# Graph network, last two edge passes: TensorE waits for a tabled count of landed tiles instead of for its own group's tiles

## The chip, the cores and the metric

The kernel runs on one core of a Trainium2 chip. The metric is the device time of one execution in microseconds (us); it is the median of several runs, and one further execution was taken with the hardware profiler, from which all rows of the trace come.

## What is computed

Four graph layers run on 6,250 nodes (256 features, float32) and 100,000 edges (`src`, `dst`; the edges come sorted by `dst`): two attention layers, a continuous-filter convolution, a relational layer and a gated normalised sum. The change touches the edge passes of the last two. In the reference they read

```python
# relation layer (L2)
hW = jnp.einsum('nd,rde->rne', h, weight)
msg = hW[edge_type, src]
m = jax.ops.segment_sum(msg, dst, num_segments=num_nodes)
...
# last layer (L3), row = src, col = dst
msg = gated[col] * edge_values[:, None]
out = jax.ops.segment_sum(msg, row, num_segments=n)
sumnorm = jax.ops.segment_sum(edge_values * r_D[col, 0], row, num_segments=n)
```

`src` is drawn evenly over the nodes; `dst` is 6250 times the square of an even draw, so that low node numbers have many edges and high ones few.

## The kernel before

The edges lie in TP = 784 tiles of P = 128, and the nodes in NT = 50 node tiles of 127. A scatter-add is done as a sum of matmuls: a tile of gathered rows (128 edges) is multiplied with a one-hot matrix that says for each edge which node of a node tile it goes to. A tile of edges that reaches into a new node tile is needed once for each of them; each such pair is a **slot**, and there are S = 832 slots. Slot s works for node tile nrow[s] and reads edge tile s - nrow[s], so slots run ahead of tiles by one with every new node tile: at the end slot 831 reads tile 782. Work goes in groups of GROUP = 8: NTG = 98 groups of tiles, NG = 104 groups of slots.

Both edge passes (`phase_rel_messages`, names `rel_...`, and `phase_source_sums`, names `so_...`, `source_ring`, `source_sums`) share one shape. Each engine has its own program, written out by hand, and semaphores tie them:

- ACT copies the row numbers of tile group g into `idx` (L2216, L2809), once the gather that used this buffer before has landed.
- POOL issues 8 indirect DMAs for tile group g (L2179, L2771) into a ring of RING = 12 (relation) or RING2 = 9 (last) groups. Its DMAs increment `x_ready[r]`. Before it overwrites a ring place it waits for `o_ready` of slot group g - LAG, with LAG = 5, or g - LAG2, with LAG2 = 2.
- VectorE (DVE) builds the one-hots of slot group g + 1 (L2231 in one instruction, L2834 in eight), then adds the 8 products of slot group g to the node sums (L2245, L2844). It loads 8 values of `nrow` into registers for each; the last pass does so twice a group, ahead of the one-hots and ahead of the adds, into one set of registers.
- TensorE (PE) in `sums(g)` loads 8 ring places from `tring` into registers, waits for the one-hots, and makes 8 products (L2198, L2789; a float32 product shows as two rows of weights and two of data). Each half group increments `o_ready`. In the relation pass three half-group PSUM buffers turn over, in the last pass 8 banks, one per slot, so that TensorE's first half there waits for the first four adds of the group before.

What sets the order around the change is this wait ahead of `sums(g)` on TensorE:

```python
pe.wait_ge(x_ready[r], it * (16 * GROUP) + 16 * GROUP)
sums(it * RING + r, r)
```

So slot group g waits until tile group g has landed, for all g below 98; the slot groups 98 to 103 wait for no tiles. When VectorE has made the last add, a block ends with all engines meeting, and the next phase starts (the gate's projection after the relation pass, `phase_last` after the last pass). VectorE also builds the tables `tring` and `nrow` in `phase_index` (by `dst`, for the relation pass) and `phase_order` (by `src`, for the last one).

Of the kernel before, what the change touches and what calls it, by code (L numbers as in the profile page):

```python
# [175 lines left out]
def phase_index(nc, m, d, sem):  # L176
# [15 lines left out]
    with ExitStack() as ctx:  # L192
# [25 lines left out]
        with nc.Block() as block:  # L218
# [12 lines left out]
            def _(dve):  # L231
# [76 lines left out]
                ch.link(nc.vector.tensor_tensor(ring[:, 0, :], ring[:, 0, :], ring[:, 1, :], ALU.add))  # L308
                ch.do(nc.vector.tensor_copy(m.tring[:, 0:S], ring[:, 0, :]))
                ch.do(nc.vector.tensor_copy(m.nrow[:, 0:S], tmp[0:1, :]))  # L310


                ch.do(nc.vector.tensor_copy(start[:], tmp[:, 0:S:P]))
# [1833 lines left out]
def phase_rel_messages(nc, m, d, x, sem):  # L2147
# [6 lines left out]
    x_ready = [sem(f"rows_gathered{b}") for b in range(RING)]  # L2154
    idx_ready = sem("index_ready")
    idx_pass = sem("index_pass")
    hot_ready = sem("onehot_ready")
    o_ready = sem("slot_sums")
    acc_done = sem("added")
# [2 lines left out]
    with ExitStack() as ctx:  # L2162
# [5 lines left out]
        with nc.Block() as block:  # L2168
# [15 lines left out]
            @block.tensor  # L2184
            def _(pe):
                regs = [pe.alloc_register(f"pe_rel_{j}") for j in range(GROUP)]

                def sums(g, r):
                    b = r % 2
                    pe.load(regs, m.tring[0:1, bass.ds(g * GROUP, GROUP)])  # L2190
                    ts = [pe.snap(t, min_val=0, max_val=RING * GROUP - 1) for t in regs]
                    pe.wait_ge(hot_ready, g + 1)
                    for j in range(GROUP):
                        n = g * PART + j // PER
                        q = (r * PART + j // PER) % BUFS
                        if j % PER == 0:
                            pe.wait_ge(acc_done, n * PER + PER)
                        ins = nc.tensor.matmul(psO[q][j % PER // (PER // 2)][:, j % (PER // 2), :], hot[b][:, j, :], x[:, bass.ds(ts[j] * D, D)], start=True, stop=True)  # L2198
                        if j % PER == PER - 1:
                            ins.then_inc(o_ready, 1)  # L2200
                with pe.Fori(0, NG // RING - 1) as it:
                    for r in range(RING):
                        pe.wait_ge(x_ready[r], it * (16 * GROUP) + 16 * GROUP)
                        sums(it * RING + r, r)
                for g in range(NG - NG % RING - RING, NG):
                    if g < NTG:
                        pe.wait_ge(x_ready[g % RING], g // RING * (16 * GROUP) + 16 * GROUP)
                    sums(g, g % RING)
                pe.wait_ge(o_ready, NG * PART)

            @block.scalar
            def _(act):
                def index(g, r, turn):
                    if not (isinstance(g, int) and g < RING):
                        act.wait_ge(x_ready[r], turn * (16 * GROUP))
                    nc.scalar.copy(idx[r][:], m.rel_tile[:, bass.ds(g * GROUP, GROUP)]).then_inc(idx_ready, 1)  # L2216
                tile_turns(act, index, 1)

            @block.vector
            def _(dve):  # L2220
# [495 lines left out]
def phase_source_sums(nc, m, d, x, sem):  # L2716
# [7 lines left out]
    rows_ready = sem("slot_rows_loaded")  # L2724
    idx_ready = sem("index_ready")
    idx_pass = sem("index_pass")
    places_ready = sem("places_spread")
    hot_ready = sem("onehot_ready")
    o_ready = sem("slot_sums")
# [14 lines left out]
    with ExitStack() as ctx:  # L2744
        sb, ps = buf_maker(nc, ctx, "so")
        edges = sb("edges", [P, TP * PAY])
        nrow = sb("nrow", [1, SR], I32)
        tring = sb("tring", [1, SR], I32)
        shift = sb("shift", [P, NT])
        places = sb("places", [P, NT, P])  # L2750
        idx = [sb(f"idx{b}", [P, GROUP], I32) for b in range(RING2)]
# [2 lines left out]
        with nc.Block() as block:  # L2754
# [21 lines left out]
            @block.tensor  # L2776
            def _(pe):
                regs = [pe.alloc_register(f"pe_so_{j}") for j in range(GROUP)]
                pe.wait_ge(rows_ready, 32)

                def sums(g, b):
                    pe.load(regs, tring[0:1, bass.ds(g * GROUP, GROUP)])
                    ts = [pe.snap(t, min_val=0, max_val=RING2 * GROUP - 1) for t in regs]
                    pe.wait_ge(hot_ready, g + 1)
                    for j in range(GROUP):
                        if j % PER == 0:

                            pe.wait_ge(acc_done, g * GROUP + j + PER)
                        ins = nc.tensor.matmul(psO[j][:, 0:K], hot[b][:, j, :], x[:, bass.ds(ts[j] * K, K)], start=True, stop=True)  # L2789
                        if j % PER == PER - 1:  # L2790
                            ins.then_inc(o_ready, 1)
                with pe.Fori(0, NTG // RING2 // 2) as it:
                    for r in range(2 * RING2):
                        pe.wait_ge(x_ready[r % RING2], it * (32 * GROUP) + (r // RING2 + 1) * (16 * GROUP))
                        sums(it * (2 * RING2) + r, r % 2)
                for g in range(NTG - NTG % (2 * RING2), NG):
                    if g < NTG:
                        pe.wait_ge(x_ready[g % RING2], (g // RING2 + 1) * (16 * GROUP))
                    sums(g, g % 2)
                pe.wait_ge(o_ready, NG * PART)  # L2800

            @block.scalar
            def _(act):
                act.wait_ge(order_ready, 16)

                def index(g, r, turn):
                    if not (isinstance(g, int) and g < RING2):
                        act.wait_ge(x_ready[r], turn * (16 * GROUP))
                    nc.scalar.copy(idx[r][:], edges[:, bass.ds(g * (GROUP * PAY), GROUP * PAY)].rearrange("p (j k) -> p j k", k=PAY)[:, :, 0]).then_inc(idx_ready, 1)  # L2809
                turns(act, index, 1)  # L2810

            @block.vector
            def _(dve):
                v = nc.vector
                regs = [dve.alloc_register(f"dve_so_{j}") for j in range(GROUP)]
                v.memset(m.sums[:], 0.0).then_inc(zeroed, 1)
                v.tensor_scalar(shift[:], m.iota[:, 0:NT], float(P), None, ALU.mult).then_inc(shift_ready, 1)
                dve.sem_inc(acc_done, GROUP)
                dve.wait_ge(shift_ready, 1)
                v.tensor_tensor(places[:], m.iota[:, 0:P].unsqueeze(1).to_broadcast([P, NT, P]), shift[:].unsqueeze(2).to_broadcast([P, NT, P]), ALU.add).then_inc(places_ready, 1)  # L2820
                dve.wait_ge(places_ready, 1)
                dve.wait_ge(zeroed, 1)
                dve.wait_ge(rows_ready, 32)
                dve.wait_ge(order_ready, 16)
                flat = places[:].rearrange("p n e -> p (n e)")

                def numbers(g):
                    dve.load(regs, nrow[0:1, bass.ds(g * GROUP, GROUP)])
                    return [dve.snap(n, min_val=0, max_val=NT - 1) for n in regs]

                def onehots(g, b, ns):
                    for j in range(GROUP):
                        t = nc.s_assert_within(g * GROUP + j - ns[j], 0, TP - 1, skip_runtime_bounds_check_because="buckets are numbered so that this is an edge tile's number")
                        ins = v.tensor_scalar(hot[b][:, j, :], flat[:, bass.ds(ns[j] * P, P)], edges[:, bass.ds(t * PAY + 2, 1)], edges[:, bass.ds(t * PAY + 1, 1)], ALU.is_equal, ALU.mult)  # L2834
                    ins.then_inc(hot_ready, 1)

                def adds(g, ns):
                    for j in range(GROUP):
                        if j % PER == 0:
                            dve.wait_ge(o_ready, g * PART + j // PER + 1)  # L2840

                        dve.wait_ge(acc_done, g * GROUP + j + GROUP)
                        to = m.sums[:, bass.ds(ns[j] * K, K)]
                        v.tensor_tensor(to, to, psO[j][:, 0:K], ALU.add).then_inc(acc_done, 1)  # L2844

                def group(g, b, more=True):

                    if more:
                        onehots(g + 1, 1 - b, numbers(g + 1))
                    adds(g, numbers(g))  # L2850
                onehots(0, 0, numbers(0))
                with dve.Fori(0, NG // 2 - 1) as it:
                    for b in range(2):
                        group(it * 2 + b, b)
                group(NG - 2, 0)
                group(NG - 1, 1, False)
                dve.wait_ge(acc_done, S + GROUP)

# [125 lines left out]
def build(nc, d, w, out):  # L2984
    m = Mem()
    with ExitStack() as ctx:
        def sb(name, shape, dt=F32):
            return ctx.enter_context(nc.sbuf_tensor(name, shape, dt))
# [12 lines left out]
        def eb(name, shape, dt=F32):  # L3001
            return edge_ctx.enter_context(nc.sbuf_tensor(name, shape, dt))
        m.loc = eb("loc", [P, SX])
        m.tring = eb("tring", [1, SX], I32)
        m.nrow = eb("nrow", [1, SX], I32)
        m.pos = eb("pos", [P, TP], I32)
        m.pay = eb("pay", [P, TP, PAY])

# [161 lines left out]
```

## Time and profile before

| | us |
|---|---|
| runs | 7715.18, 7710.42, 7712.72 |
| median | 7712.72 |
| profiled execution, its own time | 7716.48 |
| its span, first to last instruction | 7714.7 |
| relation pass, first gather to last add | 5289.1 to 6316.9 |
| last pass, first gather to last add | 6479.2 to 7532.8 |
| busy over the span: PE, DVE, ACT, POOL | 5501.5, 4562.5, 1960.2, 4805.4 |

The spans of the two passes are read from the first row of the gathers and the last row of the adds. Together they take 27% of the time. An engine is counted busy only while an instruction of it computes or, for POOL, describes a DMA; a register load, a semaphore wait and a branch leave no row and show as idle time ahead of the next row, whose releaser is then "issue" or whatever semaphore came last.

### The profile page before, as it was taken

What the parts mean: (1) busy time and instruction counts of PE and PEld (TensorE: products, weight loads), DVE (VectorE), ACT (ScalarE), POOL (GpSimd) and SP (SyncE); (2) the same over time, 40 slices, a digit from 0 to 9 for tenths busy, and PEclk for the clock granted to TensorE, in tenths of its full rate; (3) what the DMA queues carried; (4) which work ended last, traced back from release to release, by engine and by line L of the source; (5) the groups of instructions that cost most, each with busy time, mean ns of one, the idle gap of its engine ahead of it and who ended that gap; (6) DMA issues with size and microseconds to landing.
All of it is one profiled execution on the core that took longest, in us unless ns stands there. A gap on an engine that the chain in (4) does not pass through costs nothing. (4 is left out here: it accounts for less than half of the span.)

```text
span 7714.7 us, 103020 instructions
## 1 busy us (share of the span) xinstructions
PE 5501.5 (71%) x21382; PEld 3803.1 (49%) x21383; DVE 4562.5 (59%) x9626; ACT 1960.2 (25%) x6454; POOL 4805.4 (62%) x4886
## 2 busy tenths in 40 slices
PE   5768999977699999675677778995565554565550
PEld 2235565544566555454666664443444443444440
DVE  5357777777577777767344443223444456666667
ACT  0036666632366666332000001110000001000002
POOL 0017777765477777655777776777777733777750
PEclk8578999986889999866555557997777777777775
DMA  0075455522345545223111112433333323333322
GB/s 17 25 164 143 136 135 135 136 73 63 122 133 135 135 134 137 59 66 91 31 31 31 31 31 76 125 118 103 105 105 105 105 87 117 106 105 105 105 76 69
DMA packets 431408, 733.88 MB, mean 95 GB/s; under 512 B 112552, under 2 KB 278777, under 8 KB 429718
## 3 DMA queue, kind: packets, MB, share of 16 engines
q0 software_dynamic: 212352, 484.47, 24.0%
q1 hardware_dynamic: 217510, 246.12, 10.5%
q14 instruction: 141, 1.16, 0.1%
q8 instruction: 57, 0.93, 0.1%
q10 hardware_dynamic: 1348, 1.21, 0.0%
HBM read 610.03 MB, written 121.40 MB: 95 GB/s over the span
## 5 line engine op out<-in xcount | busy, mean ns | idle before, releaser
L746 POOL DMA_INDIRECT at_x<-table,at_idx x1664 | 1575.6, 947 | 587.8 <-issue 525.6
L821 PE MATMUL at_psO<-at_x,at_main 128*128 128x273 f32 x3328 | 1032.2, 434 | 157.3 <-DVE agg L1011 156.7
L1242 POOL DMA_INDIRECT order<-pay,pos x784 | 823.1, 1050 | 391.1 <-issue 245.0
L2789 PE MATMUL so_psO<-source_ring,so_hot 128*128 x1664 | 603.8, 540 | 489.2 <-issue 381.4
L2771 POOL DMA_INDIRECT source_ring<-gated_rows,so_idx x784 | 749.0, 955 | 286.5 <-issue 232.7
L2023 POOL DMA_INDIRECT conv_x<-conv_table,conv_idx x784 | 755.7, 964 | 263.7 <-issue 238.7
L2198 PE MATMUL rel_psO<-rel_ring,rel_hot 128*128 x1664 | 596.6, 536 | 449.4 <-issue 257.6
L2179 POOL DMA_INDIRECT rel_ring<-rel_table,rel_idx x784 | 741.3, 946 | 250.5 <-issue 237.9
L821 PEld LDWEIGHTS at_psO<-at_x,at_main 128*128 128x128 f32 x3328 | 606.3, 200 | 529.7 <-issue 412.1
L1011 DVE TENSOR_TENSOR agg<-agg,at_psO 128x273 f32 x1664 | 725.7, 436 | 221.6 <-DVE agg L1011 169.3
L2789 PEld LDWEIGHTS so_psO<-source_ring,so_hot 128*128 128x128 f32 x1664 | 458.9, 283 | 634.0 <-issue 531.4
L2198 PEld LDWEIGHTS rel_psO<-rel_ring,rel_hot 128*128 128x128 f32 x1664 | 455.7, 281 | 590.6 <-issue 492.2
L2245 DVE TENSOR_TENSOR rel_sums<-rel_sums,rel_psO 128x256 f32 x832 | 350.0, 421 | 449.5 <-PE rel_psO L2198 350.6
L907 ACT COPY at_row<-at_psO 1x273 f32<-1x273 f32 x1664 | 523.3, 373 | 345.9 <-PE at_psO L821 345.6
L1002 DVE TENSOR_TENSOR at_x<-at_x,at_psE 128x512 f32<-128x512 f32 x832 | 560.8, 674 | 0.8 <-issue 0.8
L2844 DVE TENSOR_TENSOR source_sums<-source_sums,so_psO 128x257 f32 x832 | 351.9, 423 | 245.1 <-PE so_psO L2789 135.4
L2060 PE MATMUL conv_psO<-conv_msg,conv_hot 128*128 x1664 | 381.8, 421 | 157.7 <-DVE conv_hot L2099 149.5
L2047 PE MATMUL conv_psF<-w_radial,conv_attr 12*128 12x64 f32 x1568 | 359.2, 419 | 161.7 <-DVE conv_prod L2109 134.0
L2060 PEld LDWEIGHTS conv_psO<-conv_msg,conv_hot 128*128 128x128 f32 x1664 | 362.8, 331 | 176.6 <-issue 176.3
L2047 PEld LDWEIGHTS conv_psF<-w_radial,conv_attr 12*128 12x128 f32 x1568 | 341.3, 326 | 179.6 <-DVE conv_prod L2109 131.9
L799 PE MATMUL at_psA<-a_ij,at_fullT 128*128 x3328 | 402.5, 257 | 0.0
L799 PEld LDWEIGHTS at_psA<-a_ij,at_fullT 128*128 128x128 f32 x3328 | 395.0, 195 | 0.0
(487 smaller groups left out, 8292.5 us busy)
## 6 DMA issues: line engine op xcount, KB each, us to landing
at_place<-places SPq DMA_DIRECT2D x208, 256.0 KB, 3.7
rel_table<-cr_rows SPq DMA_DIRECT2D x50, 1024.0 KB
at_x<-table,at_idx POOLq DMA_INDIRECT x1664
pj_x<-table SPq DMA_DIRECT2D x20, 640.0 KB, 4.2
order<-pay,pos POOLq DMA_INDIRECT x784, 2.1
conv_x<-conv_table,conv_idx POOLq DMA_INDIRECT x784, 2.4
rel_ring<-rel_table,rel_idx POOLq DMA_INDIRECT x784, 2.7
source_ring<-gated_rows,so_idx POOLq DMA_INDIRECT x784, 2.8
```

The costliest lines, as they stand in the source:

```text
L746: pool.indirect_dma_start(x[b][:, j, 0:TABW], None, d.table[0:NR, :], bass.IndirectOffsetOnAxis(ap=idx[b][:, j:j + 1], axis=0)).then_inc(x ...
L799: nc.tensor.matmul(psA[:, j, :], fullT[:, j, :], m.a_ij[:, bass.ds(ns[j] * (2 * H) + H, H)], start=False, stop=False, skip_group_check=True)
L821: ins = nc.tensor.matmul(psO[j % BANKS][:, 0:AGG], main[b % 2][:, j, :], x[b][:, j, 0:AGG], start=True, stop=True)
L1011: nc.vector.tensor_tensor(to, to, psO[j % BANKS][:, 0:AGG], ALU.add).then_inc(acc_done, 1)
L1242: pool.indirect_dma_start(d.order[0:TP * P, :], bass.IndirectOffsetOnAxis(ap=m.pos[:, t:t + 1], axis=0), m.pay[:, t, :], None).then_inc(pl ...
L2023: pool.indirect_dma_start(x[b][:, j, :], None, d.conv_table[:, :], bass.IndirectOffsetOnAxis(ap=idx[b][:, j:j + 1], axis=0)).then_inc(x_re ...
L2047: ins = nc.tensor.matmul(psF[b][:, j, :], attr[b][:, j * P:(j + 1) * P], m.w_radial[:], start=True, stop=True)
L2060: ins = nc.tensor.matmul(psO[b][j // (GROUP // 2)][:, j % (GROUP // 2), :], hot[b][:, j, :], msg[:, bass.ds(ts[j] * K, K)], start=True, st ...
L2179: pool.indirect_dma_start(x[:, at:at + D], None, d.rel_table[:, :], bass.IndirectOffsetOnAxis(ap=idx[r][:, j:j + 1], axis=0)).then_inc(x_r ...
L2198: ins = nc.tensor.matmul(psO[q][j % PER // (PER // 2)][:, j % (PER // 2), :], hot[b][:, j, :], x[:, bass.ds(ts[j] * D, D)], start=True, st ...
L2771: pool.indirect_dma_start(x[:, at:at + K], None, d.gated[:, :], bass.IndirectOffsetOnAxis(ap=idx[r][:, j:j + 1], axis=0)).then_inc(x_ready ...
L2789: ins = nc.tensor.matmul(psO[j][:, 0:K], hot[b][:, j, :], x[:, bass.ds(ts[j] * K, K)], start=True, stop=True)
```

## The change

A new table `needed` has one number for each slot group: how many edge tiles must have landed before all its 8 slots can be computed. That is the tile of its last slot plus one (slot number + 1 - nrow). The relation pass's table is written in `phase_index`, the last pass's at the start of `phase_source_sums`. ACT, which waited for each gather to land before it copied the next row numbers over that buffer, now also adds 8 to a new semaphore `gathered` after each such wait, and goes on doing so for the last ring of tile groups. TensorE no longer waits on `x_ready`; it loads `needed[g]` into a register and waits for `gathered` to reach it. In the last pass TensorE's loop is now 52 turns of two slot groups (before: 5 turns of 18, and 14 groups written out), and VectorE keeps the node tile numbers of a group in one of two sets of registers from the one-hots to the adds, so that they are loaded once.

```diff
--- before.py
+++ after.py
...
+                ch.do(nc.vector.tensor_scalar(m.needed[:], slot[0:1, 3, GROUP - 1:S:GROUP], 1.0, None, ALU.add))
...
+    gathered = sem("tiles_gathered")
...
                 def sums(g, r):
                     b = r % 2
                     pe.load(regs, m.tring[0:1, bass.ds(g * GROUP, GROUP)])
+                    tiles = pe.value_load(m.needed[0:1, bass.ds(g, 1)], min_val=1, max_val=TP)
                     ts = [pe.snap(t, min_val=0, max_val=RING * GROUP - 1) for t in regs]
                     pe.wait_ge(hot_ready, g + 1)
+                    pe.wait_ge(gathered, tiles)
                     for j in range(GROUP):
                         n = g * PART + j // PER
...
                 with pe.Fori(0, NG // RING - 1) as it:
                     for r in range(RING):
-                        pe.wait_ge(x_ready[r], it * (16 * GROUP) + 16 * GROUP)
                         sums(it * RING + r, r)
                 for g in range(NG - NG % RING - RING, NG):
-                    if g < NTG:
-                        pe.wait_ge(x_ready[g % RING], g // RING * (16 * GROUP) + 16 * GROUP)
                     sums(g, g % RING)
                 pe.wait_ge(o_ready, NG * PART)
 
             @block.scalar
             def _(act):
-                def index(g, r, turn):
-                    if not (isinstance(g, int) and g < RING):
-                        act.wait_ge(x_ready[r], turn * (16 * GROUP))
+                def index(g, r):
                     nc.scalar.copy(idx[r][:], m.rel_tile[:, bass.ds(g * GROUP, GROUP)]).then_inc(idx_ready, 1)
-                tile_turns(act, index, 1)
+
+                def landed(r, turn):
+
+                    act.wait_ge(x_ready[r], turn * (16 * GROUP) + 16 * GROUP)
+                    act.sem_inc(gathered, GROUP)
+                for r in range(RING):
+                    index(r, r)
+                with act.Fori(0, NTG // RING - 1) as it:
+                    for r in range(RING):
+                        landed(r, it)
+                        index(it * RING + r + RING, r)
+                for g in range(NTG - NTG % RING - RING, NTG):
+                    landed(g % RING, g // RING)
+                    if g + RING < NTG:
+                        index(g + RING, g % RING)
 
...
+    gathered = sem("tiles_gathered")
+    need_ready = sem("needed_tiles")
...
+        needed = sb("needed", [1, NG], I32)
...
+                pe.wait_ge(need_ready, 1)
 
                 def sums(g, b):
                     pe.load(regs, tring[0:1, bass.ds(g * GROUP, GROUP)])
+                    tiles = pe.value_load(needed[0:1, bass.ds(g, 1)], min_val=1, max_val=TP)
                     ts = [pe.snap(t, min_val=0, max_val=RING2 * GROUP - 1) for t in regs]
                     pe.wait_ge(hot_ready, g + 1)
+                    pe.wait_ge(gathered, tiles)
...
-                with pe.Fori(0, NTG // RING2 // 2) as it:
-                    for r in range(2 * RING2):
-                        pe.wait_ge(x_ready[r % RING2], it * (32 * GROUP) + (r // RING2 + 1) * (16 * GROUP))
-                        sums(it * (2 * RING2) + r, r % 2)
-                for g in range(NTG - NTG % (2 * RING2), NG):
-                    if g < NTG:
-                        pe.wait_ge(x_ready[g % RING2], (g // RING2 + 1) * (16 * GROUP))
-                    sums(g, g % 2)
+                with pe.Fori(0, NG // 2) as it:
+                    for b in range(2):
+                        sums(it * 2 + b, b)
                 pe.wait_ge(o_ready, NG * PART)
...
-                regs = [dve.alloc_register(f"dve_so_{j}") for j in range(GROUP)]
+                regs = [[dve.alloc_register(f"dve_so{b}_{j}") for j in range(GROUP)] for b in range(2)]
...
+                v.scalar_tensor_tensor(out=needed[:], in0=m.iota[0:1, GROUP - 1:S:GROUP], scalar=1.0, in1=nrow[:, GROUP - 1:S:GROUP], op0=ALU.add, op1=ALU.subtract).then_inc(need_ready, 1)
...
-                def numbers(g):
-                    dve.load(regs, nrow[0:1, bass.ds(g * GROUP, GROUP)])
-                    return [dve.snap(n, min_val=0, max_val=NT - 1) for n in regs]
+                def numbers(g, b):
+                    dve.load(regs[b], nrow[0:1, bass.ds(g * GROUP, GROUP)])
+                    return names(b)
+
+                def names(b):
+                    return [dve.snap(n, min_val=0, max_val=NT - 1) for n in regs[b]]
...
                 def group(g, b, more=True):
 
                     if more:
-                        onehots(g + 1, 1 - b, numbers(g + 1))
-                    adds(g, numbers(g))
-                onehots(0, 0, numbers(0))
+                        onehots(g + 1, 1 - b, numbers(g + 1, 1 - b))
+                    adds(g, names(b))
+                onehots(0, 0, numbers(0, 0))
                 with dve.Fori(0, NG // 2 - 1) as it:
                     for b in range(2):
                         group(it * 2 + b, b)
...
+        m.needed = eb("needed", [1, NG], I32)
```

On TensorE, at the start of the loop of the last pass, these rows stood from the loop's head to the first product of a slot group (`so_tring`: ring places; ISA rows are waits, register moves and address work, without names):

```order
L2792 ISA
L2782 ISA
L2782 TENSOR_LOAD so_tring
L2783 ISA
L2788 REGISTER_ALU
L2789 ISA
L2789 MATMUL so_psO<-source_ring,so_hot 128x257
```

and these stand there now:

```order
L2811 ISA
L2799 TENSOR_LOAD so_tring
L2800 ISA
L2800 TENSOR_LOAD so_needed
L2800 ISA x2
L2801 ISA
L2807 REGISTER_ALU
L2808 ISA
L2808 MATMUL so_psO<-source_ring,so_hot 128x257
```

The wait that stood ahead of the load of `so_tring` is gone, and a second load (`so_needed`) stands between it and the first product. The relation pass reads the same with `rel_...` names.

On VectorE, in the last pass, from the last one-hot of group g + 1 to the first add of group g, the rows were:

```order
L2834 TENSOR_SCALAR so_hot<-so_places,so_edges 128x128
L2828 ISA
L2828 TENSOR_LOAD so_nrow
L2829 ISA
L2840 REGISTER_ALU
L2842 REGISTER_ALU
L2844 ISA
L2844 TENSOR_TENSOR source_sums<-source_sums,so_psO 128x257
```

and are now:

```order
L2864 TENSOR_SCALAR so_hot<-so_places,so_edges 128x128
L2859 ISA
L2870 REGISTER_ALU
L2872 ISA
L2874 ISA
L2874 TENSOR_TENSOR source_sums<-source_sums,so_psO 128x257
```

The second load of `so_nrow` is gone; the one ahead of the one-hots stays.

## Rows read from the trace of the kernel before

**Rows 1.** Costliest groups, relation pass: us busy, mean ns, idle before, releasers.

```profile
L2179 POOL DMA_INDIRECT rel_ring<-rel_table,rel_idx x784 | 741.3, 946 | 250.5 <-issue 237.9 <-ACT rel_idx L2216 12.0 <-PE rel_psO L2198 0.6
```

**Rows 2.** Timeline, relation pass: start, length (us), engine, [idle before <-releaser].

```profile
5303.18 5.51 PE L2198 MATMUL rel_psO<-rel_ring,rel_hot 128*128 x16 [37.43 <-DVE rel_hot L2231]
...
6100.75 0.20 ACT L2216 COPY rel_idx<-rel_tile 128x8 int32 x1 [9.82 <-DMA rel_ring<-rel_table,rel_idx]
6101.85 5.40 PE L2198 MATMUL rel_psO<-rel_ring,rel_hot 128*128 x16 [4.59 <-issue]
6105.60 4.36 DVE L2245 TENSOR_TENSOR rel_sums<-rel_sums,rel_psO 128x256 f32 x8 [3.58 <-PE rel_psO L2198]
6111.87 5.40 PE L2198 MATMUL rel_psO<-rel_ring,rel_hot 128*128 x16 [4.61 <-DVE rel_hot L2231]
```

**Rows 3.** Timeline, the end of the relation pass.

```profile
6261.84 5.40 PE L2198 MATMUL rel_psO<-rel_ring,rel_hot 128*128 x16 [4.65 <-DVE rel_hot L2231]
6265.06 2.11 DVE L2245 TENSOR_TENSOR rel_sums<-rel_sums,rel_psO 128x256 f32 x4 [3.56 <-PE rel_psO L2198]
...
6267.96 0.95 POOL L2179 DMA_INDIRECT rel_ring<-rel_table,rel_idx  x1 [0.30 <-issue]
6269.98 1.22 DVE L2231 TENSOR_TENSOR rel_hot<-rel_psI,loc 128x1024 f32<-128x1024 f32 x1 [0.47 <-issue]
...
6273.33 8.59 PE L2198 MATMUL rel_psO<-rel_ring,rel_hot 128*128 x32 [6.08 <-issue]
...
6295.59 4.01 PE L2198 MATMUL rel_psO<-rel_ring,rel_hot 128*128 x16 [0.63 <-DVE rel_hot L2231]
...
6301.62 4.01 PE L2198 MATMUL rel_psO<-rel_ring,rel_hot 128*128 x16 [2.03 <-DVE rel_hot L2231]
...
6314.82 2.11 DVE L2245 TENSOR_TENSOR rel_sums<-rel_sums,rel_psO 128x256 f32 x4 [0.21 <-DVE rel_sums L2245]
6321.29 0.39 SPq L2606 DMA_DIRECT2D ga_wsup<-in_s_W  x1
```

**Rows 4.** Costliest groups, last pass.

```profile
L2771 POOL DMA_INDIRECT source_ring<-gated_rows,so_idx x784 | 749.0, 955 | 286.5 <-issue 232.7 <-ACT so_idx L2809 48.0 <-PE so_psO L2789 5.8
```

**Rows 5.** Timeline, the end of the last pass.

```profile
7449.71 5.42 PE L2789 MATMUL so_psO<-source_ring,so_hot 128*128 x16 [4.51 <-issue]
...
7459.69 5.88 PE L2789 MATMUL so_psO<-source_ring,so_hot 128*128 x16 [4.56 <-issue]
...
7465.85 0.94 POOL L2771 DMA_INDIRECT source_ring<-gated_rows,so_idx  x1 [0.30 <-issue]
...
7471.13 5.30 PE L2789 MATMUL so_psO<-source_ring,so_hot 128*128 x16 [5.55 <-issue]
...
7490.03 3.07 DVE L2834 TENSOR_SCALAR so_hot<-so_places,so_edges 128x128 f32 x8 [0.96 <-issue]
7493.97 0.42 DVE L2844 TENSOR_TENSOR source_sums<-source_sums,so_psO 128x257 f32 x1 [0.87 <-issue]
...
7499.70 3.06 DVE L2834 TENSOR_SCALAR so_hot<-so_places,so_edges 128x128 f32 x8 [1.35 <-issue]
7503.73 4.38 DVE L2844 TENSOR_TENSOR source_sums<-source_sums,so_psO 128x257 f32 x8 [0.97 <-issue]
...
7509.07 3.07 DVE L2834 TENSOR_SCALAR so_hot<-so_places,so_edges 128x128 f32 x8 [0.97 <-issue]
...
7524.94 5.42 PE L2789 MATMUL so_psO<-source_ring,so_hot 128*128 x16 [4.20 <-DVE source_sums L2844]
7528.34 2.12 DVE L2844 TENSOR_TENSOR source_sums<-source_sums,so_psO 128x257 f32 x4 [1.32 <-PE so_psO L2789]
7530.67 2.12 DVE L2844 TENSOR_TENSOR source_sums<-source_sums,so_psO 128x257 f32 x4 [0.21 <-DVE source_sums L2844]
```

**Rows 6.** Timeline, the start of the last pass.

```profile
6486.22 6.82 DVE L2820 TENSOR_TENSOR so_places<-iota,so_shift 128x6400 f32<-128x6400 f32 x1
6486.84 7.03 POOL L2771 DMA_INDIRECT source_ring<-gated_rows,so_idx  x1 [0.30 <-issue]
...
6498.45 5.24 PE L2789 MATMUL so_psO<-source_ring,so_hot 128*128 x16 [61.07 <-DVE so_hot L2834]
```

**Rows 7.** VectorE's small operation nearest in size to the new ones.

```profile
7540.04 0.19 DVE L2938 TENSOR_SCALAR la_no_node<-mask 128x49 f32<-128x49 f32 x1 [7.24 <-PEq L2754]
```

More of the change, by code:

```diff
@@ L2804, in _, with index, landed @@
                 act.wait_ge(order_ready, 16)
-                def index(g, r, turn):
-                    if not (isinstance(g, int) and g < RING2):
-                        act.wait_ge(x_ready[r], turn * (16 * GROUP))
+                def index(g, r):
                     nc.scalar.copy(idx[r][:], edges[:, bass.ds(g * (GROUP * PAY), GROUP * PAY)].rearrange("p (j k) -> p j k", k=PAY)[:, :, 0]).then_inc(idx_ready, 1)
-                turns(act, index, 1)
+                def landed(r, turn):
+                    act.wait_ge(x_ready[r], turn * (16 * GROUP) + 16 * GROUP)
+                    act.sem_inc(gathered, GROUP)
+                for r in range(RING2):
+                    index(r, r)
+                with act.Fori(0, NTG // RING2 - 1) as it:
+                    for r in range(RING2):
+                        landed(r, it)
+                        index(it * RING2 + r + RING2, r)
+                for g in range(NTG - NTG % RING2 - RING2, NTG):
+                    landed(g % RING2, g // RING2)
+                    if g + RING2 < NTG:
+                        index(g + RING2, g % RING2)
             @block.vector
```

## The prediction

> **What bounds the kernel now.** I read first the grouped instructions of the two edge passes. In the relation pass POOL issues 784 gathers; their busy time and the idle time ahead of them, without the 12.0 us of the start, make (741.3 + 238.5) / 784 = 1.250 us each, 10.0 us per tile group [rows 1]. Almost all of that idle time is "issue", 0.3 us between two gathers; for TensorE's progress POOL waited 0.6 us in all in the relation pass and 5.8 us in the last pass [rows 1, 4]. So both passes run at POOL's pace, and nothing that TensorE or VectorE does sooner changes the start of a gather.
>
> Next I read the timeline in the middle. ACT is released by a landing at 6100.75, TensorE starts its group at 6101.85, works 5.40 us and starts the next at 6111.87: its turn is POOL's 10.0 us, and it is idle for 4.6 us of it. VectorE's adds follow 3.75 us behind TensorE's start and take 4.36 us [rows 2]. Both engines idle in every turn, and nothing there is on the path but the gathers.
>
> That ends with the last gather. In the relation pass it is issued at 6267.96; TensorE starts slot group 97 at 6273.33, and the groups 98 to 103 still follow: VectorE's last add ends at 6314.82 + 2.11 = 6316.93, and 4.4 us later the next phase issues its first load [rows 3]. So 43.6 us of the pass are a tail of seven groups at 6.03 us (TensorE's starts at 6295.59 and 6301.62). In the last pass the last gather is issued at 7465.85, group 97 starts at 7471.13 and the last add ends at 7530.67 + 2.12 = 7532.79: a tail of 61.7 us [rows 5]. Its pace is VectorE's: the adds of two groups in succession start at 7493.97 and 7503.73, the one-hots at 7490.03, 7499.70 and 7509.07, so 9.5 us a group on average. That is eight one-hots 3.07, eight adds 4.38, and two gaps, 0.87 to 0.97 ahead of the adds and 0.96 to 1.35 ahead of the one-hots, where the registers are loaded (1.35 with the loop's branch).
>
> **What the change does to the tails.** A slot group needs its last slot's number + 1 - nrow tiles. The node tiles follow from the reference's draws. For the relation pass (by dst) the slots 807, 815, 823 and 831 work for the node tiles 46, 47, 48 and 49, so the groups 100 to 103 need 762, 769, 776 and 783 tiles, which is 96, 97, 97 and 98 tile groups. For the last pass (by src) nrow is 47, 48, 48 and 49, which gives 761, 768, 776 and 783 tiles: 96, 96, 97 and 98 groups. Today slot group g waits for tile group g. In the middle of a pass TensorE only works further ahead in slots, which buys nothing while POOL sets the pace. At the last landing only slot group 103 is left for certain, where seven are left now.
>
> **Relation pass, worked forward.** Slot group 101 needs the 97th tile group, for which TensorE starts at 6261.84 today; its adds go from 6265.06 to 6269.5, and the one-hots of 103 from 6269.98 to 6271.2, all as in today's rows of another group [rows 3]. TensorE ends group 101 at 6267.2. It then loads registers twice; one load is hidden in 0.63 us today (the idle time at 6295.59), so I take 1.3 us for both, and group 102 starts at 6268.5, its adds 3.2 us later (6265.06 - 6261.84), from 6271.7 to 6276.2. TensorE is free at 6273.9, the last tiles have landed at about 6272.3 (1.0 us before today's start at 6273.33, as ACT's row stands 1.1 us ahead of TensorE's in the middle [rows 2]), and group 103 starts at 6275.2. Its adds run from 6278.4 to 6282.9. Against 6316.93 that is **34.0 us** less. Bounds: if each load costs TensorE what it costs VectorE at most (0.97 us, none hidden), three groups lose 1 us each, 31; if the second costs nothing, 36.
>
> **Last pass, worked forward.** Slot group 100 needs the 96th tile group, TensorE's start at 7449.71 today [rows 5]. Its adds start 3.4 us later (7528.34 - 7524.94), at 7453.1, and end at 7457.6. VectorE then loads once (0.96), makes the one-hots of 102 until 7461.7, and without the second load adds group 101 from 7461.9 to 7466.3; one-hots of 103 from 7467.3 to 7470.4; adds of 102 from 7470.6 to 7475.0. TensorE's group 103 needs the first four of these added, so it starts at 7473.0 (the last tiles have landed by 7470.1, 1.0 us before today's 7471.13), its adds begin 3.4 us later and take 4.45: the end is at 7480.8. Against 7532.79 that is **52.0 us** less. For this VectorE must keep up before: with one gap it needs 3.07 + 4.38 + 0.96 to 1.35 + 0.2, about 8.8 us a group, while 104 slot groups in the time of 98 tile groups ask for one in 10.0 x 98 / 104 = 9.4. It can. Where two slot groups hang on one landing it falls behind by 8.8 us and makes 1.2 us good with each following landing, which takes 8 groups; such pairs are 17 groups apart. If the removed load saves nothing, VectorE goes at 9.5 against 9.4 asked for and is never clear of the backlog: 87 groups at 9.52 behind the first 17 at 10.0 put the last add near 7493, 40 us less. Upper bound 54, with TensorE's group 103 starting on the landing.
>
> **What it adds.** Per slot group one register load and one more semaphore wait on TensorE, behind which stand only its own products. They lie in its idle 4.6 us, except in the tails, where they are counted. The landing now reaches TensorE over ACT; ACT is idle 9.8 of 10.0 us [rows 2], and TensorE's first load has moved ahead of the wait, so this is no later than today. ACT's own waits are the same landings as before, so POOL gets its numbers at the same time. Two small VectorE operations: the table in the index phase is on the path and costs what an operation on 49 elements does, 0.19 us [rows 7]. The one in the last pass delays the first one-hots by as much, which the second landing hides. At the start of that pass there is one more thing to see: while VectorE built `so_places` from two tables in SBUF (6.82 us), a gather took 7.03 us instead of 0.955 [rows 6, 4]. The new operation there is of the same kind but has 104 elements, so it can hold POOL for 0.2 us at most, between 0 and 0.2 of the path. The Trainium skill (SBUF — State Buffer, Who interferes with whom) says that a two-input VectorE operation with both inputs in SBUF contends with GpSimd for the shared ports, and that tensor_scalar can too. The trace agrees on the long operation; it does not on the 832 one-hots, beside which the gathers' mean stays at 0.955. By the rule a one-hot of 0.38 us (3.07 / 8) that met a gather would hold it too, but their number does not change, so neither does the sum.
>
> **Sum.** 34.0 + 52.0 - 0.2 - 0.1 = 85.7 us. The profiled execution took 7716.48 and would take 7630.8; the median of the runs is 3.8 us below it, so 7627.
>
> **Rivals.** (1) *VectorE's cadence in the last pass does not fall*, since the gap ahead of the adds is a wait or an issue time that stays without the load. For it: that gap also shows a semaphore wait for TensorE in places. Against it: it is 0.87 to 0.97 in the tail, where TensorE is done. The last pass gives 40 instead of 52: 7639. (2) *TensorE becomes the bound*, the case on the slower side. The second load and a wait on a register's value would have to stretch its turn. It works 5.4 us and idles at least 0.63 in the tail, 6.0 together; the 104 turns of the relation pass lie between 5303.18 and 6316.93, 9.75 us each, and those of the last pass between 6498.45 and 7532.79, 9.95 each [rows 2, 3, 5, 6]. If a turn comes to more than that, the pass is slower than today; at 10.75 us they lose 104 and 83 us, 7900. That asks for over 3.7 us more per turn, where a load on VectorE shows 0.97. (3) *The shorter loop.* TensorE's loop in the last pass goes back 52 times instead of 5. On VectorE, which has such a loop, the branch shows as 1.35 against 0.96, 0.4 us [rows 5]; on TensorE two turns have 2 x (9.95 - 6.0) = 7.9 us to spare, and a stall of 10 us at each branch would cost 52 x 2.1 = 109 us in that pass, which with the 34 of the other makes 7788. The Trainium skill (Runtime: NRT & Kernel Launch, Instruction fetch mechanics) says that a taken branch out of the fetched window stalls the engine until its target is fetched; VectorE's 0.4 us says that a loop of two groups does not pay that here. (4) *The change does not do what it says*: the count reaches TensorE late in the tail, or slot group 103 is not the only one left, and the tails stay: 7713.
>
> **Chances and range.** The forecast 0.82, rival 1 0.10, rival 2 0.03, rival 3 0.02, rival 4 0.03. The bounds of the forecast give 31 + 40 to 36 + 54, so 7623 to 7642; with 3 us of scatter between runs (7710.42 to 7715.18) 7620 to 7643, which leaves out the rivals 2 to 4 and little else. Since about 0.2%, 15 us, is what a measurement of this kernel can tell from no change: faster 0.92, same 0.03, slower 0.05.
>
> **What would show it.** Right: POOL still at 1.25 us a gather; between the last landing and the last add about 11 us in either pass (now 44 and 62); no idle time of more than 0.3 us ahead of the adds in the last pass's backlog; TensorE twice a pass two groups in succession without waiting. Wrong: a gap ahead of L2874 that stays near 0.9 (rival 1), TensorE's turns without idle time (2), idle time in every second turn (3), or POOL waiting for TensorE by more than the 0.6 and 5.8 us of now, which would move every later gather.

## The result and the profile after

The changed kernel takes 7633.68 us (median of 4 runs, 7627.78 to 7634.63) against 7711.57 us for the kernel before (4 runs): ratio 0.9898, 95% interval 0.9881 to 0.9915, 78 us less. Forecast were 7627 and 86 us less. The same kernel, run once more among the experiments, took 7619.66 us (ratio 0.9884, 0.9867 to 0.9900). The profiled execution has a span of 7632.6 us, 82.1 less than before.

The grouped instructions of the two passes say whether the gathers kept their pace, the first row as in [rows 1], the last as in [rows 4]:

```profile
L2181 POOL DMA_INDIRECT rel_ring<-rel_table,rel_idx x784 | 742.4, 947 | 250.6 <-issue 236.8 <-ACT rel_idx L2215 12.0 <-PE rel_psO L2202 1.8
...
L2787 POOL DMA_INDIRECT source_ring<-gated_rows,so_idx x784 | 750.0, 957 | 286.1 <-issue 238.0 <-ACT so_idx L2821 47.5 <-PE so_psO L2808 0.6
```

They did: (742.4 + 250.6 - 12.0) / 784 = 1.251 us each, and POOL waits for TensorE 1.8 and 0.6 us in all, where it was 0.6 and 5.8. The end of the relation pass in the timeline, against [rows 3]:

```profile
6264.40 9.25 PE L2202 MATMUL rel_psO<-rel_ring,rel_hot 128*128 x32 [4.62 <-DVE rel_hot L2244]
...
6271.36 0.94 POOL L2181 DMA_INDIRECT rel_ring<-rel_table,rel_idx  x1 [0.30 <-issue]
...
6277.49 5.40 PE L2202 MATMUL rel_psO<-rel_ring,rel_hot 128*128 x16 [3.84 <-issue]
...
6283.04 2.11 DVE L2258 TENSOR_TENSOR rel_sums<-rel_sums,rel_psO 128x256 f32 x4 [0.85 <-PE rel_psO L2202]
6292.52 0.39 SPq L2619 DMA_DIRECT2D ga_wsup<-in_s_W  x1
```

Slot groups 101 and 102 run back to back on one landing (32 rows in one piece; they start 3.04 us after the issue of the last gather that they need), and only group 103 follows the last landing. From the last gather's issue to the last add's end there are 13.8 us now, where there were 49.0. But the next phase's first load comes 7.4 us after the last add, not 4.4. The end of the last pass, against [rows 5]:

```profile
7421.54 7.55 PE L2808 MATMUL so_psO<-source_ring,so_hot 128*128 x24 [4.54 <-ACTq L2826]
...
7430.28 3.07 DVE L2864 TENSOR_SCALAR so_hot<-so_places,so_edges 128x128 f32 x8 [0.97 <-issue]
...
7433.59 4.39 DVE L2874 TENSOR_TENSOR source_sums<-source_sums,so_psO 128x257 f32 x8 [0.24 <-issue]
...
7444.77 2.00 PE L2808 MATMUL so_psO<-source_ring,so_hot 128*128 x8 [3.49 <-DVE source_sums L2874]
...
7449.50 2.12 DVE L2874 TENSOR_TENSOR source_sums<-source_sums,so_psO 128x257 f32 x4 [0.21 <-DVE source_sums L2874]
7458.72 0.37 SPq L2929 DMA_DIRECT2D la_a<-in_s_a  x1
```

The gap ahead of the adds is 0.24 us instead of 0.87, and group 103 waits for VectorE's adds, no longer for a landing. The last gather there is issued at 7438.46, so 13.2 us are left of 66.9.

I read the same marks (first and last gather, last add, next phase's first load) in every profile and cut the span by them. "Tail" is the stretch from the last gather's issue to the last add's end, "gate" the phase between the two passes:

| us | first gather at | gathers | tail | to next load | gate | gathers | tail | to next load | rest |
|---|---|---|---|---|---|---|---|---|---|
| before | 5289.1 | 978.9 | 49.0 | 4.4 | 157.9 | 986.6 | 66.9 | 7.2 | 174.7 |
| changed | 5291.3 | 980.1 | 13.8 | 7.4 | 158.3 | 987.6 | 13.2 | 7.1 | 173.9 |
| changed, again | 5282.9 | 978.7 | 12.8 | 5.1 | 156.6 | 986.7 | 13.2 | 7.1 | 174.1 |

The tails give 35.2 + 53.8 = 89.0 us. Back go 3.0 at the end of the relation pass, 2.2 in the two stretches of gathers and 2.2 ahead of the first one; the other columns together give 0.5 more, which makes 82.1. Of the 2.2 us ahead of the first gather only 0.2 can be the change's (its new table operation in the index phase took 0.23 us): that mark stands between 5278.3 and 5291.3 over the twelve profiles of this study, and the one of the changed kernel was the latest. Scatter in that part, which the change hardly touches, is also 8.4 of the 15.5 us between the two profiles of the changed kernel, whose medians are 7633.7 and 7619.7.

### The profile page after: what moved, and what is told of

It reads as the page before. It is cut to its first block and busy times, and to the rows that moved or that the text cites. A ratio compares the mean times of both kernels' runs of the same rounds, so it can differ in the third digit from the quotient of the medians.

```text
span 7632.6 us, 104169 instructions
## 1 busy us (share of the span) xinstructions
PE 5462.2 (72%) x21382; PEld 3774.1 (49%) x21383; DVE 4560.7 (60%) x9628; ACT 1962.9 (26%) x6454; POOL 4813.3 (63%) x4886
## 3 DMA queue, kind: packets, MB, share of 16 engines
q1 hardware_dynamic: 217510, 246.12, 10.5%
## 5 line engine op out<-in xcount | busy, mean ns | idle before, releaser
L2808 PE MATMUL so_psO<-source_ring,so_hot 128*128 x1664 | 584.6, 525 | 455.1 <-ACTq L2826 270.0
L2181 POOL DMA_INDIRECT rel_ring<-rel_table,rel_idx x784 | 742.4, 947 | 250.6 <-issue 236.8
L2202 PE MATMUL rel_psO<-rel_ring,rel_hot 128*128 x1664 | 576.9, 522 | 437.6 <-ACTq L2220 222.3
L1012 DVE TENSOR_TENSOR agg<-agg,at_psO 128x273 f32 x1664 | 725.2, 436 | 222.3 <-DVE agg L1012 169.1
L2808 PEld LDWEIGHTS so_psO<-source_ring,so_hot 128*128 128x128 f32 x1664 | 442.2, 273 | 597.5 <-issue 501.7
```

The source lines that it names most:

```text
L1012: nc.vector.tensor_tensor(to, to, psO[j % BANKS][:, 0:AGG], ALU.add).then_inc(acc_done, 1)
L2181: pool.indirect_dma_start(x[:, at:at + D], None, d.rel_table[:, :], bass.IndirectOffsetOnAxis(ap=idx[r][:, j:j + 1], axis=0)).then_inc(x_r ...
```

## Experiments

**The kernel again.** No edit.

> The changed kernel once more, unedited, to learn how far its time and its parts repeat. 7630 to 7636. In its trace: last gather to last add about 14 us in the relation pass and 13 us in the last pass, and from the last add to the next phase's first load 7.4 and 7.1 us. If the 3 us that the relation pass's end lost against before (4.4 to 7.4) are scatter, they differ here; if they come from TensorE now ending only 2.3 us ahead of VectorE, with POOL's 9.2 us drain behind it, they stand again.

Measured 7619.66, outside what I expected. Tails 12.8 and 13.2 us, and 5.1 us to the next load. So the tails repeat within about 1 us. The end of the relation pass's block, 3.0 us longer than before in the first profile, is 0.8 us longer here. What sets it is in the rows of the block's end (line of the block's `with`), for the kernel before, the changed one, and the repeat, in this order: engine queue, operation, length in ns, start in us.

```profile
L2168 POOLq DRAIN  x1: 9194/9194/9194, 6311.9 to 6311.9; - x1
...
L2168 DVEq DRAIN  x1: 17/17/17, 6317.2 to 6317.2; - x1
L2168 SPq EVENT_SEMAPHORE  x1: 17/17/17, 6321.2 to 6321.2; - x1
```

```profile
L2170 POOLq DRAIN  x1: 9194/9194/9194, 6283.1 to 6283.1; - x1
...
L2170 DVEq DRAIN  x1: 17/17/17, 6285.4 to 6285.4; - x1
L2170 SPq EVENT_SEMAPHORE  x1: 17/17/17, 6292.4 to 6292.4; - x1
```

```profile
L2170 POOLq DRAIN  x1: 9194/9194/9194, 6270.1 to 6270.1; - x1
L2170 DVEq DRAIN  x1: 17/17/17, 6274.6 to 6274.6; - x1
```

POOL waits for the last product, and only then drains, for 9.2 us; the engines are released when that ends (6311.9 + 9.2 = 6321.1, 6283.1 + 9.2 = 6292.3). VectorE is done 2.3 to 5.3 us after the drain starts and waits for it. So the block ends 9.4 us after TensorE's last product, as long as the adds end within that time. It holds beyond these three: in the ten profiles of kernels in which POOL waits for the last product, the next phase's first load comes 9.6 us after that product in all twenty block ends, while the adds end 2.3 to 5.3 us after it. What differs between the two profiles is when TensorE ends, 11.5 us after the last gather's issue in the first and 8.3 in the repeat: the last landing was counted after 5.9 against 4.3 us, and the 16 products of group 103 took 5.40 us at a mean granted clock of 0.72 (part of them at the 1.2 GHz level) against 3.72 us at 1.00 (2.4 GHz).

**The old numbers through the new table.** Relation pass (the last pass likewise):

```diff
-ch.do(nc.vector.tensor_scalar(m.needed[:], slot[0:1, 3, GROUP - 1:S:GROUP], 1.0, None, ALU.add))
+ch.do(nc.vector.tensor_scalar(m.needed[:], m.iota[0:1, GROUP - 1:S:GROUP], 1.0, float(TP), ALU.add, ALU.min))
```

> Everything of the change stays (table, count on ACT, register wait, short loop, two register sets), but the table holds what the wait of before asked for: 8 (g + 1) tiles, at most 784. If the gain is in the numbers of the table, it is gone: the seven slot groups stand behind the last landing again. Kept are some 5 us, since the last pass's tail of seven groups goes at 8.8 instead of 9.5 us, and 0.8 us of reaction per pass: 7703 to 7707. If the loop, the loads or the way of waiting carried the gain: near 7634.

Measured 7705.11 (ratio 0.9994, 0.9984 to 1.0004). The tails are back, 47.9 and 62.7 us. So the gain is in the numbers, but for the 4.2 us that are left (in the tails 1.1 and 4.2); the second load, the register wait, the hop over ACT and the loop of two groups cost nothing that shows.

**One pass alone.** The other pass's function is that of the kernel before.

> Only the relation pass is changed, the last pass is that of before. Theory of two separate tails: last gather to last add falls by 35 us, and the end of the block gives 3 back, so 32 less, 7679 to 7681. If the passes shared the gain in another way (an earlier phase that meets other work), the two halves would not add up to 78 us.

> Only the last pass is changed, the relation pass is that of before. Two separate tails: 54 us less in this one, nothing given back, 7657 to 7659, and together with the relation pass alone the whole 78 to 85 us. Otherwise they do not add up.

Measured 7677.54 (ratio 0.9960) and 7654.11 (0.9930). Measured beside them, the kernel before had 7709.34 and the changed one 7619.66. The two passes alone give 31.8 and 55.2 us, together 87.0 (I had expected 78 to 85); both at once give 89.7. They add up to within 2.7 us, less than the scatter of the phases ahead. In the profiles the relation pass's tail is 12.3 us with 5.4 to the next load, the last pass's 14.2 us.

**VectorE loads twice again.**

```diff
-                    adds(g, names(b))
+                    adds(g, numbers(g, b))
```

> The changed kernel, but VectorE in the last pass loads the node tile numbers again ahead of the adds. If the load is the 0.9 us gap there, VectorE goes at 9.5 us a group, 9.4 are asked for, its backlog is never worked off, and the last add comes 8 to 12 us later: 7642 to 7646. If the gap was a wait that needs no load, the time stays at 7634.

Measured 7632.31, below the 7642 to 7646 that I expected. Against the changed kernel's 7619.66 that is 12.7 more, against its first 7633.68 nothing, so the medians don't decide; the profiles do. The last pass's tail is 24.6 us, against 13.2 in both profiles of the changed kernel and 14.1 with the long loop below; the other parts agree within the scatter (gathers 978.8 and 987.0, relation tail 12.6). In its timeline the gap is back, and the adds that wait behind it are late:

```profile
7430.63 3.07 DVE L2864 TENSOR_SCALAR so_hot<-so_places,so_edges 128x128 f32 x8 [0.97 <-issue]
7434.57 0.42 DVE L2874 TENSOR_TENSOR source_sums<-source_sums,so_psO 128x257 f32 x1 [0.87 <-issue]
```

The gap is the load (0.87 against 0.24 us), and 0.6 us per group are worth 11.5 us at the end, because without them VectorE clears its backlog between two pairs of slot groups and with them it does not: ahead of the last pass's products TensorE waited 16 times for a landing and 90 times for VectorE's adds, in the changed kernel 65 and 46 times.

**The registers alone**, in the kernel before:

> The kernel before with one part of the change: VectorE's two register sets in the last pass, one load a group. POOL sets the pace, so only the tail of seven groups gains, 7 x 0.7 = 5 us: 7706. If VectorE's loads had held the pass up in the middle: 50 us or more less. If the gap was no load: 7711.

Measured 7706.96 (0.9998, 0.9988 to 1.0007), no difference that can be told. In the profile the last pass's tail falls from 66.9 to 63.6 us, 3.3 of the 5 expected. Only five of the seven turns have the load on the path, those between the first adds of group 97 and of group 102: 44.3 us instead of 47.6, 8.9 instead of 9.5 a turn. Ahead of the adds of groups 97 and 103 VectorE waits for TensorE in either kernel (2.9 and 1.6 us, before 2.8 and 1.3), and the load is hidden there. One edit is worth 3 us before the new counts and 11 behind them.

**TensorE's long loop**, 5 turns of 18 slot groups and 14 groups written out, in the changed kernel:

> The changed kernel with TensorE's loop of the last pass as before: 5 turns of 18 slot groups and 14 groups written out, instead of 52 turns of two. If the branch and the fetch behind it hide in TensorE's idle 4 us: no difference, 7631 to 7637. If the short loop costs something at each of its 52 branches that reaches the path, this is faster by that; if it saves fetches of code that held the gathers or the landings up, it is slower by a few us.

Measured 7627.05 (7619.46 to 7627.66), below the 7631 to 7637 that I expected and between the two medians of the changed kernel; tails 12.6 and 14.1 us, gathers 986.9 us. No cost of the short loop reaches the path: the stall of the rule that the prediction weighed (the Trainium skill, Runtime: NRT & Kernel Launch, Instruction fetch mechanics) does not show here.

**One tile group later.** All entries of both tables 8 higher, at most 784.

> The changed kernel with every entry of both tables 8 tiles higher, at most 784, so that each slot group waits for one tile group more than it needs. Theory of the tails: nothing in the middle; in the relation pass the slot groups 101, 102 and 103 all hang on the last landing, two more turns of 6.0 us behind it, 12 us; in the last pass 102 and 103, one more turn of 8.8 less the 2 us by which VectorE is late now, 7 us. 7634 + 19 = 7653. If a later count delayed the whole pass by one turn of the gathers: 10 us in each, and the tails as long as now.

Measured 7702.09, not 7653: nearly the whole gain was gone. The tails did about what was expected (23.8 and 25.1 us, 10 to 11 more in the first where I had 12, and 12 more in the second where I had 7), but the last pass's gathers took 1046.1 us instead of 986.7, which I had not looked for. The waits of its last pass, and POOL's timeline in its first turns:

```profile
POOL source_ring L2789 <- PE so_psO L2810: 63.1, 14, 6.9
```

```profile
6551.03 0.95 POOL L2789 DMA_INDIRECT source_ring<-gated_rows,so_idx  x1 [6.92 <-PE so_psO L2810]
...
6567.61 0.94 POOL L2789 DMA_INDIRECT source_ring<-gated_rows,so_idx  x1 [6.89 <-PE so_psO L2810]
...
6584.15 0.95 POOL L2789 DMA_INDIRECT source_ring<-gated_rows,so_idx  x1 [6.85 <-PE so_psO L2810]
```

POOL now waits for TensorE before a gather group, 6.9 us each time, so that a turn takes 16.6 us instead of 10.0. The cause is the ring: gather group g may start when slot group g - 2 has its first half (LAG2 = 2), and with the higher entry that slot group needs tile group g - 1 landed, so gathers and products alternate instead of overlapping. It lasts from group 9, the first that reuses a ring place, to about group 17, where the slots have run one group ahead of the tiles. Nine times 6.9 is 62 of the 63.1 us. In the relation pass, with LAG = 5, the gathers stayed at 979.0. In these first 17 groups the needed counts, in whole tile groups, are still the old ones (the slots have not yet run ahead by 8 tiles), so the wait of before had less than one tile group of slack there, and the change keeps it.

**POOL leaves early.** Without the last line of POOL's program in both passes:

```diff
                 turns(pool, gather, 1)
-                pool.wait_ge(o_ready, NG * PART)
```

> The changed kernel without POOL's last wait in both passes (for the last products); all engines still meet at the end of the block, and VectorE's last wait stands. Theory: POOL's drain of 9.2 us now starts only behind the last product and ends 7 us after the last add, in both passes; without the wait it starts behind the last gather, runs beside TensorE's and VectorE's last groups, and the next phase starts 0.3 to 0.5 us after the last add: 7 us less in either pass, 7619 to 7621. Rival: the drain waits for something that only ends with the block (or for the landings, and then takes 9.2 us from there): no change, or 3 us less.

> The kernel before without the same two waits. The relation pass ended 4.4 us after its last add there, the last pass 7.2 us. Theory: both fall to 0.3 to 0.5 us, 4 + 7 = 11 us less, 7700 to 7702. Rival as for the changed kernel: no change.

Measured 7609.20 (7608.46 to 7610.94; ratio 0.9870, 0.9854 to 0.9885), the fastest here, and for the kernel before 7697.53 (0.9983, 0.9974 to 0.9992), 12.8 less than the 7710.28 measured beside it (by the two block ends of the profiles 3.9 + 6.7 = 10.6). Both lie below what I expected, 7619 to 7621 and 7700 to 7702; the first expectation went out from 7634. In both, both blocks end 0.5 us after the last add. The relation pass's end with the wait gone, in the changed kernel:

```profile
L2170 POOLq DRAIN  x1: 24197/24197/24197, 6246.9 to 6246.9; - x1
...
L2170 DVEq DRAIN  x1: 17/17/17, 6274.4 to 6274.4; - x1
L2170 SPq EVENT_SEMAPHORE  x1: 17/17/17, 6274.6 to 6274.6; - x1
```

The drain begins while gathers are still being issued and ends at 6246.9 + 24.2 = 6271.1, 3.3 us ahead of VectorE's: hidden. But it does not get cheaper. The last gather's row is

```profile
6260.93 0.95 POOL L2181 DMA_INDIRECT rel_ring<-rel_table,rel_idx  x1 [0.30 <-issue]
```

It ends at 6260.93 + 0.95 = 6261.88, 9.2 us before the drain does, and so it is in all four blocks without the wait (both kernels, both passes): the drain takes 9.2 us from the end of POOL's last gather, or from the end of its wait where it has one. It does not count from the landings (here ACT counts the last at 6265.7), as my rival had it. Against the changed kernel the gain is 10.5 us by medians of two separate measurements (7619.66 and 7609.20), not the 14 of my expectation, which took the block end of 7.4 us from the first profile. By the profiles the two block ends give 4.6 + 6.6 = 11.2 us against the repeat, and the tails were 0.5 and 1.9 us longer in this execution.

## Why the prediction was right, and where it was off

The direction, the mechanism and the size held: POOL sets the pace, the middle of the passes gains nothing, and all of the gain but some 4 us is slot groups that no longer stand behind the last landing. The old numbers through the new table take it away again, which shows it.

*Relation pass, 34.0 us.* Measured 35.2 between the last gather and the last add (13.8 us left; the working gave 14.9), 36.2 in the repeat. The term of 1.3 us for two register loads on TensorE was wrong in size: groups 101 and 102 follow each other with no gap at all, and group 103 starts 0.2 us after ACT has counted the last landing (6277.3). And the working let TensorE start as late after a landing as before, where it starts 0.8 us sooner (below). In this one profile the last landing was counted 5.9 us after the last gather's issue (seven of the other profiles: 4.1 to 4.8), which ate part of that.

*The step that failed* is "VectorE's last add ends at 6314.82 + 2.11 = 6316.93, and 4.4 us later the next phase issues its first load", which I took as a constant behind the tail. It is not one: the block ends 9.4 us after TensorE's last product, because POOL waits for that product and then drains for 9.2 us. Before, VectorE's adds ended 5.3 us behind the last product and hid more than half of it. Now, at 2.3 and in the repeat 4.5 us behind it, less is hidden, so 3.0 of the 35.2 us went back (0.8 of the 36.2 in the repeat). It was not in my sum, nor in a rival. From the last gather to the next load, which is what counts, the pass gave 32.2 and 35.4 us. That the forecast of 34.0 lies between them is partly luck: what the working left out here lengthens the time, and the two terms above that it took too large shorten it.

*Last pass, 52.0 us.* Measured 53.8. The working put the last add at 15.0 us behind the last gather's issue, it is 13.2. Of the 1.8 us, 0.8 are TensorE's earlier start of group 103 (6.3 us behind the last gather, in the working 7.1), and 1.0 its products: the adds begin 2.4 us after that start, not the 3.4 taken from the kernel before, where the 16 products of the last group took 5.42 us at a mean granted clock of 0.69; now each half took 2.00 us, at 1.00. The pace without the second load was taken as 8.8 us and is 8.9 (the mean of 8.7 and 9.1 in the profile of the registers alone).

*What it adds, 0.3 us.* The operation in the last pass took 0.33 us, not 0.2, and the one in the index phase 0.23, not 0.19. The first delays nothing: the first one-hot starts 1.02 us after `so_places` is done, before and now, and the gather that `so_places` held ends 0.8 us after it in both. The gathers' stretches were 1.2 and 1.0 us longer in the first profile, and in the repeat 0.2 shorter and 0.1 longer: scatter.

*Rival 1* (VectorE's cadence does not fall, 12 us of the gain) had its price right, 11.5 us, and its condition wrong: the gap was the load. With the load back the tail is 42.3 us shorter than before, where the rival had 40. *Rivals 2 and 3* (TensorE as the bound, the short loop) did not come about; TensorE has idle time before nearly every group. The wait for the landing now shows as one for ACT's count, 222.3 us in 54 waits in the relation pass:

```profile
PE rel_psO L2202 <- ACTq L2220: 222.3, 54, 6.3
```

TensorE starts 3.04 us after the issue of the last gather that it needs (6264.40 after a gather one turn of 10.0 us ahead of the one at 6271.36), where it took 3.87 (6261.84 after the one a turn ahead of 6267.96 [rows 3]). It is so all along the pass: over the starts of the relation pass with more than 3 us of idle time ahead of them the median is 3.13 us (92 starts), and was 3.95 (98). So the hop over ACT costs less than having the load ahead of the wait saves; no run has the one without the other. "No later than today" in the working was 0.8 us too careful.

Of the signs, "about 11 us in either pass" between the last landing and the last add came out as about 8 and 9, for the same terms. "Twice a pass two groups in succession" was a slip: 104 slot groups hang on 98 tile groups, which makes six such pairs a pass.

My claim that nothing TensorE or VectorE does sooner changes the start of a gather held for this change. What TensorE does later is another matter, and I had not looked there: the shift by one tile group cost 59 us of gathers in the last pass.

## What to carry to other kernels

When a producer runs at a fixed pace through a ring, ask how many consumer steps stand behind its last item, and whether each truly needs it: seven groups, at 6 and 9 us, were worth 1.0 to 1.2% here, and the middle nothing. A wait by need also has to be checked from the other side, where the producer waits for the consumer: one tile group of unneeded lateness cost 59 us through a lag of two. And read the queues' own rows at the end of a block (drain, branch, semaphore), not the last busy row: the engine that finishes last may be one that only waited.

## What the runs showed that I had not expected

POOL's drain at the end of a block with 784 gathers takes 9.19 us (both passes, before and after) if POOL first waits for the last product, and it holds all engines. If POOL goes into it straight from its gathers, it ends 9.2 us after the last of them, in the relation pass 3.3 us before VectorE's end. What the 9.19 us consist of was not tried; in other blocks of this kernel the drain has other lengths (0.03 to 8.6 us).

The phases ahead of the two passes differ by up to 13 us (5278.3 to 5291.3 at the first gather) between executions of kernels that are the same there but for one operation of 0.23 us, which is as much as the last experiment's gain. The cut of the span by stage tells parts of 1 us that the medians cannot.
